# Experts: two tiles' products made in the gates' stage; mixer: convolution passes between the chunks' reads

## The chip, the cores and the metric

The kernel runs on one core of one Trainium2 chip. Its engines are TensorE (PE), VectorE (DVE), ScalarE (ACT), GpSimd (POOL) and SyncE (SP). The metric is the time of one execution on the device, in microseconds (us); less is better.

## The reference

One layer on a stream `x` of 8 x 512 x 128 float32 (4096 tokens): attention, experts, mixer, experts again. Each adds to the stream. The change touches the last three.

```
x = x + attention(layernorm(x))          # 16 heads of 64, rel. positions, top-k, 3 powers
x = x + experts(layernorm(x))            # top-1 of 8 experts, capacity tokens / 8
x = x + mixer(layernorm(x))
x = x + experts(layernorm(x))

# experts: logits = xt @ wg; mask = one_hot(argmax); drop the tokens beyond the capacity
#          gate = sum(softmax * mask); out = gate * (W[e] @ x + b[e])

# mixer:   z, xBC, dt = split(u @ W_in.T)
#          xBC = silu(causal convolution of 4 taps over time (xBC) + conv_b)
#          x, B, C = split(xBC)            # 128, 16, 16 channels; 8 heads of 16
#          y = ssd(x * dt, A * dt, B, C)   # chunks of time, decays inside, states between them
#          y = concat(y + x * Dskip, z); layernorm; out = y @ W_out.T
```

## The kernel before

Tokens lie in 32 tiles of 128. `k.X` is the stream, `k.XNT` the normed stream, transposed. Every engine runs its own program in its own order, written out by hand; semaphores join them. `bank` is PSUM: `ps[0]` to `ps[7]`, each 128 x 512. The program is a row of stages (`nc.Block`); each ends when all engines have reached its end.

**Experts** (`experts`, run twice) has two stages. In the *gates' stage* VectorE derives for all tiles the winning expert, its place in the queue and the gate (`b.gate8`). TensorE takes part once: when the mask is there (`step`) it multiplies it with `r.after` and `r.ones` into `ps[4]` and `ps[5]`, and VectorE goes on from these to the last gate (L1230 to L1238). In the *products' stage* TensorE multiplies each tile with all 8 expert matrices, as two products of 128 x 512: `q = 0` (experts 0 to 3, "near") and `q = 1` (4 to 7, "far"). Tile t uses banks 0 and 1 for even t, 2 and 3 for odd t. VectorE scales the near half with the gates (L1351), ScalarE the far half (L1314), VectorE adds them (L1343), GpSimd sums over experts and adds to the stream. Between the products TensorE transposes the gates of four tiles (`turn_gates`, L1259; ScalarE keeps them, L1302) and makes the bias product from them (L1282).

**Mixer** (`mixer`): the main stage walks over 8 batches of 512 tokens, each of 4 chunks of 128. One *step* has batch `front` enter (projections, convolution, silu), batch `cur` in its chunks, batch `back` in its norm and output, and `done` in the norm for the experts. On TensorE a chunk c has a `first_half` (the decays' differences, L1561, then the *transposes* of x and B and the product of B and C into bank `T1`, L1569 to L1571) and a `second_half` (L1580, L1584). TensorE's order in a step:

```
first_half 0, project x z bc, first_half 1, mean, second_half 0, from_start, first_half 2,
output, second_half 1, turn, first_half 3, second_half 2, square_sums, second_half 3,
logits, from_states
```

On VectorE `before(cur, c)`, the *chunk's read*, takes chunk c out of `T1` (L1843 to L1849; the last of them raises `turned_used`, on which the transposes of chunk c + 1 wait) and then multiplies the decays by the result, in two instructions L1853 (`weights`, on which `second_half` c waits). `convolution(front)` makes 4 taps for x and for B and C together, so 8 instructions (L1815 for tap 0, L1818 for taps 1 to 3). ScalarE turns the last tap's sums into tanh and half (`squash`, L1722, L1723), and VectorE makes of them silu (L1828 to L1833), on which the transposes of the next step's chunk 0 wait. GpSimd in a step: `spread` 2, the squares, `spread` 3, `spread` 0 of the next batch, `bias`, rstd, `spread` 1.

Of the kernel before, what the change touches and what calls it, by code (L numbers as in the profile page):

```python
# [16 lines left out]
P = 128  # L17
# [37 lines left out]
def bcast(ap, dims):  # L55

    return bass.AP(ap.tensor, ap.offset, [list(ap.ap[0])] + [list(d) for d in dims])
# [1026 lines left out]
CONV = 4  # L1084
# [63 lines left out]
def experts(nc, sem, sb, ps, k, r, tag, made=None, follow=None, gw=None, out=None, logits=None):  # L1148
    def S(n):
        return sem(f"{tag}_{n}")  # L1150
# [4 lines left out]
    near_made, far_made, far_scaled, near_scaled = (S(n) for n in ("near_made", "far_made", "far_scaled", "near_scaled"))  # L1155
# [27 lines left out]
    def v3(x):  # L1183
        return x[:, :].rearrange("p (t e) -> p t e", e=E)

    def over(x):

        return bcast(x[:, :], [[1, TILES], [0, E]])

    with nc.Block() as block:  # L1190
        @block.tensor
        def _(pe):
            pe.wait_ge(step, 1)
            nc.tensor.matmul(ps[4][:, 0:n8], r.after[:, :], b.mask[:, :], start=True, stop=True)
            nc.tensor.matmul(ps[5][:, 0:n8], r.ones[:, :], b.mask[:, :], start=True, stop=True).then_inc(counted, 1)

        @block.scalar
        def _(act):
            act.wait_ge(ex_done, 1)
            nc.scalar.activation(b.exp[:, :], b.diff[:, :], ACT.Exp).then_inc(ex_done, 1)  # L1200

        @block.vector
        def _(dve):
            chain = [0]

            def link(ins):

                chain[0] += 1
                ins.then_inc(gates, 1)
                dve.wait_ge(gates, chain[0])  # L1210

            link(nc.vector.memset(b.sum_b[:, :], 1.0))
            link(nc.vector.memset(b.sum_b[:, :].rearrange("p (e t) -> p e t", e=E)[:, :, 0:1], 0.0))
            if logits is None:
                dve.wait_ge(made.products, GROUPS)
                link(nc.vector.tensor_copy(b.logit[:, :], ps[3][:, 0:n8]))
            link(nc.vector.tensor_reduce(out=b.top[:, :], in_=v3(b.logit), axis=AX.X, op=ALU.max))
            nc.vector.tensor_tensor(v3(b.diff), v3(b.logit), over(b.top), ALU.subtract).then_inc(ex_done, 1)

            link(nc.vector.tensor_tensor(v3(b.same), v3(b.logit), over(b.top), ALU.is_equal))  # L1220
            link(nc.vector.tensor_tensor(v3(b.score), v3(b.same), bcast(r.rank[:, :], [[0, TILES], [1, E]]), ALU.mult))
            link(nc.vector.tensor_reduce(out=b.best[:, :], in_=v3(b.score), axis=AX.X, op=ALU.max))
            nc.vector.tensor_tensor(v3(b.mask), v3(b.score), over(b.best), ALU.is_equal).then_inc(step, 1)

            dve.wait_ge(ex_done, 2)
            link(nc.vector.tensor_reduce(out=b.total[:, :], in_=v3(b.exp), axis=AX.X, op=ALU.add))
            link(nc.vector.reciprocal(b.prob[:, :], b.total[:, :]))

            dve.wait_ge(counted, 1)
            link(nc.vector.tensor_copy(b.prev[:, :].rearrange("p (e t) -> p e t", e=E),  # L1230
                                       ps[5][:, 0:n8].rearrange("p (t e) -> p e t", e=E)))
            link(nc.vector.tensor_tensor_scan(out=b.sum_a[:, :], data0=b.sum_b[:, :], data1=b.prev[:, :],
                                              initial=0.0, op0=ALU.mult, op1=ALU.add))
            link(nc.vector.tensor_tensor(v3(b.loc), b.sum_a[:, :].rearrange("p (e t) -> p t e", e=E),
                                         ps[4][:, 0:n8].rearrange("p (t e) -> p t e", e=E), ALU.subtract))
            link(nc.vector.scalar_tensor_tensor(out=b.keep[:, :], in0=b.loc[:, :], scalar=float(CAP), in1=b.mask[:, :],
                                                op0=ALU.is_le, op1=ALU.mult))
            link(nc.vector.tensor_tensor(v3(b.gate8), v3(b.keep), over(b.prob), ALU.mult))  # L1238
# [3 lines left out]
    with nc.Block() as block:  # L1242
# [9 lines left out]
        @block.tensor  # L1252
        def _(pe):
            def turn_gates(i):
                if i:
                    pe.wait_ge(g_kept, i)
                for c in range(4):
                    at = (i * 4 + c) * E
                    last = nc.tensor.transpose(GT[0:E, c * P:(c + 1) * P], b.gate8[:, at:at + E], k.ident[:, :])  # L1259
                last.then_inc(g_turned, 1)  # L1260

            def late(i):
                group_turn(nc, pe, follow, i, gw.xn[:, i % 2, :], TURN, k.ident, 1)

            for i in range(GROUPS):
                par = i % 2
                if i == 0:
                    turn_gates(0)
                for c in range(4):
                    t = i * 4 + c  # L1270
                    for q in range(2):
                        if t >= 2:
                            pe.wait_ge((near_scaled, far_scaled)[q], t - 1)
                        nc.tensor.matmul(ps[2 * (c % 2) + q][:, :], k.XNT[:, t * P:(t + 1) * P],  # L1274
                                         r.we[:, q * 512:(q + 1) * 512], start=True, stop=True)\
                            .then_inc((near_made, far_made)[q], 1)
                    if c == 0:
                        pe.wait_ge(g_kept, i + 1)
                        if i:
                            pe.wait_ge(bias_added, i)  # L1280
                        for cc in range(4):
                            last = nc.tensor.matmul(BIAS[:, cc * P:(cc + 1) * P], gt[par][:, cc * P:(cc + 1) * P],  # L1282
                                                    r.eb[:, :], start=True, stop=True)
                        last.then_inc(bias_made, 1)
                    if c == 1 and follow and i >= 2:
                        late(i - 2)
                    if c == 2 and i + 1 < GROUPS:
                        turn_gates(i + 1)
                    if c == 3 and follow and i >= 2:
                        group_products(nc, pe, follow, i - 2, follow.W, k.XNT, EIGHT)  # L1290
            if follow:
                for i in range(GROUPS - 2, GROUPS):
                    late(i)
                    group_products(nc, pe, follow, i, follow.W, k.XNT, EIGHT)
# [97 lines left out]
def mixer(nc, sem, sb, ps, k, r, made, follow, gw):  # L1392
# [137 lines left out]
    with nc.Block() as block:  # L1530
# [264 lines left out]
        def _(dve):  # L1795
# [9 lines left out]
                ins.then_inc(m.link, 1)  # L1805
                return links[0]

            def convolution(j):

                at = {}  # L1810
                for tap in range(CONV):
                    for which, src, acc, weight in (("x", xp, cx, r.cwx), ("bc", bp, cb, r.cwb)):
                        if tap == 0:
                            dve.wait_ge(m.conv_in, j * 3 + (1 if which == "x" else 2))
                            done = nc.vector.tensor_scalar(acc[0][:, :], src[:, 0:N], weight[:, 0:1], None, ALU.mult)  # L1815
                        else:
                            dve.wait_ge(m.link, at[which])
                            done = nc.vector.scalar_tensor_tensor(  # L1818
                                out=acc[tap % 2][:, :], in0=src[:, tap:tap + N], scalar=weight[:, tap:tap + 1],
                                in1=acc[1 - tap % 2][:, :], op0=ALU.mult, op1=ALU.add)  # L1820
                        if tap < CONV - 1:
                            at[which] = link(done)
                        else:
                            done.then_inc(m.conv_out, 1)
# [82 lines left out]
            def body(front, cur, back, done):  # L1907
                if cur is not None:
                    before(cur, 0)
                    before(cur, 1)  # L1910
                if back is not None:
                    center(back)
                if front is not None:
                    convolution(front)
                if cur is not None:
                    before(cur, 2)
                    before(cur, 3)
                    states(cur)
                if back is not None:
                    variance(back)  # L1920
                if front is not None:
                    silu(front)
                if back is not None:
                    into_stream(back)
                if cur is not None:
                    add_up(cur)

            run_steps(body)


# [106 lines left out]
```

## Time and profile before

| | us |
|---|---|
| median of 3 runs (2867.4 to 2874.39) | 2870.75 |
| profiled execution | 2866.37 |
| its span | 2864.6 |
| to the first gates' stage (attention) | 2347.9 |
| the mixer's main stage | 2460.9 to 2775.3 |
| second gates' stage | 2775.3 to 2783.8 |
| second products' stage | 2783.8 to 2864.6 |

Times in the rows count from the start of the span. PE's float32 products show as two records each, so "x4" on L1274 is two products; the transposes of L1569 show as one. "PEclk" is the clock granted to TensorE as a share of 2.4 GHz: 1.00 or 0.50 (1.2 GHz).

### The profile page before, as it was taken

The page shows a single profiled execution, that of the slowest core. Times are in us where ns is not written, and L with a number is a line of the kernel's source. Part 1 is how long each engine was busy: PE and PEld are TensorE (multiplying, and loading weights), DVE is VectorE, ACT ScalarE, POOL GpSimd, SP SyncE. Part 2 cuts the span into 40 slices and gives each one's busy share as a digit, 9 for nine tenths or more (in the row PEclk, how much of TensorE's full clock was granted, in tenths as well). Part 3 has the DMA queues.
Part 4 walks back from the last instruction along what each step waited for, and adds up shares of the span by engine and source line. Part 5 has one row for each costly group of instructions (what it writes and reads, how often), then busy time and mean ns, then how long its engine had stood idle before and what let it go on. Part 6 is the DMA issues. An engine that isn't in the chain of part 4 may idle for free. (4 is left out here: it accounts for less than half of the span.)

```text
span 2864.6 us, 54829 instructions
## 1 busy us (share of the span) xinstructions
PE 2455.1 (86%) x16162; PEld 1364.4 (48%) x16162; DVE 2640.0 (92%) x6343; ACT 2072.3 (72%) x6299; POOL 2322.1 (81%) x2900
## 2 busy tenths in 40 slices
PE   5888888888888888888888888888888879588878
PEld 3444444544444444444444444444444445355544
DVE  7999999999999999999999999999999937577747
ACT  3788888888888888888888888888888736333325
POOL 5899999999999999999999999999999936344425
PEclk8899999999999999999999999999999979677769
DMA  4444444444444444444444444444444300000001
GB/s 128 118 122 118 118 119 121 124 123 118 120 124 118 123 120 118 119 125 125 119 118 122 118 123 120 123 119 124 121 125 118 100 15 1 1 1 1 1 1 30
DMA packets 367800, 279.65 MB, mean 98 GB/s; under 512 B 27590, under 2 KB 366608, under 8 KB 367504
## 3 DMA queue, kind: packets, MB, share of 16 engines
q1 hardware_dynamic: 366576, 274.06, 33.8%
q8 instruction: 131, 2.15, 0.3%
q10 hardware_dynamic: 928, 2.10, 0.3%
q14 instruction: 165, 1.35, 0.2%
HBM read 139.48 MB, written 136.58 MB: 96 GB/s over the span
## 5 line engine op out<-in xcount | busy, mean ns | idle before, releaser
L969 DVE MAX8 top<-work 128x8 f32<-128x512 f32 x1536 | 978.3, 678 | 0.0
L978 DVE MATCH_REPLACE8 work<-top,work 128x512 f32<-128x512 f32 x1024 | 684.4, 676 | 0.0
L1055 POOL TENSOR_TENSOR scores<-scores,cut 128x512 f32<-128x512 f32 x512 | 643.3, 1278 | 0.0
L588 PE MATMUL bank<-probs_t,u 128*64 128x512 f32 x2048 | 470.9, 602 | 11.5 <-ACT u L824 1.8
L1047 POOL TENSOR_SCALAR cut<-scores,minus_max_and_least 128x512 f32<-128x512 f32 x512 | 355.7, 695 | 46.9
L876 ACT ACTIVATE probs_of_tile<-scores,minus_max_and_least 128x512 f32<-128x512 f32 x512 | 376.4, 765 | 16.1 <-POOL scores L1055 16.0
L1068 POOL TENSOR_SCALAR probs_of_tile<-probs_of_tile,inverse 128x512 f32<-128x512 f32 x512 | 350.7, 696 | 26.9 <-DVE inverse L935 1.4
L978 DVE MATCH_REPLACE8 work<-top,scores 128x512 f32<-128x512 f32 x512 | 342.1, 676 | 0.0
L966 DVE MAX8 top<-scores 128x8 f32<-128x512 f32 x512 | 324.9, 676 | 1.1 <-ACT scores L817 1.0
L1051 POOL TENSOR_SCALAR cut<-cut 128x512 f32<-128x512 f32 x512 | 306.6, 615 | 21.6
L795 ACT ACTIVATE band<-band 128x129 f32<-128x129 f32 x512 | 155.1, 304 | 215.2 <-DMA band<-probs_scratch 214.9
L817 ACT ACTIVATE scores<-bank 128x512 f32<-128x512 f32 x512 | 274.0, 585 | 48.2 <-PE bank L637 48.1
L841 ACT ACTIVATE probs_t<-bank 128x512 f32<-128x512 f32 x512 | 281.3, 609 | 8.4 <-PE bank L684 7.4
L684 PE MATMUL bank<-identity,probs_of_tile 128*128 128x128 f32 x2048 | 273.7, 278 | 2.7 <-POOL probs_of_tile L1068 2.7
L672 PE MATMUL bank<-identity,band 128*128 128x128 f32 x512 | 109.2, 295 | 179.2 <-ACT band L804 178.2
L588 PEld LDWEIGHTS bank<-probs_t,u 128*64 128x64 f32 x2048 | 136.5, 137 | 263.9 <-issue 222.7
L588 PE MATMUL bank<-probs_t,v 128*64 128x384 f32 (+1 forms) x2048 | 255.3, 392 | 0.0
L684 PEld LDWEIGHTS bank<-identity,probs_of_tile 128*128 128x128 f32 x2048 | 238.6, 144 | 3.1 <-POOL probs_of_tile L1068 3.1
L588 PEld LDWEIGHTS bank<-probs_t,v 128*64 128x64 f32 x2048 | 124.3, 139 | 172.6 <-ACT probs_t L841 98.7
L609 PE MATMUL bank<-keys_left,qt 64*128 64x64 f32 (+3 forms) x1024 | 186.0, 440 | 1.5 <-ACT scores L817 1.4
L854 ACT ACTIVATE rel<-bank 128x254 f32<-128x254 f32 x512 | 174.4, 413 | 1.9 <-PE bank L625 1.9
L1021 POOL TENSOR_TENSOR res<-res,tmp 128x512 f32<-128x512 f32 x128 | 163.5, 1278 | 10.7
(281 smaller groups left out, 4753.4 us busy)
## 6 DMA issues: line engine op xcount, KB each, us to landing
probs_scratch<-probs_of_tile SPq DMA_DIRECT2D x256, 256.0 KB, 2.5
band<-probs_scratch SPq DMA_DIRECT2D x256, 256.0 KB, 3.1
rel_scratch<-rel SPq DMA_DIRECT2D x256, 254.0 KB, 3.0
relj<-rel_scratch SPq DMA_DIRECT2D x256, 128.0 KB, 2.3
relj<-rel_scratch SPq DMA_DIRECT2D x512, 64.0 KB, 2.4
stream<-in_L_attn_a_x SPq DMA_DIRECT2D x4, 512.0 KB, 8.8
out_stream<-stream SPq DMA_DIRECT2D x8, 256.0 KB, 2.3
wout_rows<-in_L_attn_a_Wout ACTq DMA_DIRECT2D x1, 512.0 KB, 11.8
```

Of the source, the lines that this page charges most:

```text
L588: last = nc.tensor.matmul(U[HEADS[h], lo:hi], lhs, pt[mpar][:, h, jt, lo:hi], start=(jt == 0 and lo == 0), stop=(jt == NT - 1 and step > 0))
L684: last = nc.tensor.transpose(PT[h][:, jt * P:(jt + 1) * P], t.prob[Td][:, h, HALF + jt * P:HALF + (jt + 1) * P], k.ident[:, :])
L817: nc.scalar.activation(sc[Tb][:, h, :], SC[h][:, :], ACT.Copy).then_inc(s.scores_kept, 1)
L841: nc.scalar.activation(pt[dpar][:, h, :, Td * P:(Td + 1) * P], PT[h][:, :].rearrange("p (j i) -> p j i", j=NT), ACT.Copy).then_inc(s.probs ...
L876: nc.scalar.activation(t.prob[Tx][:, h, HALF:HALF + N], sc[Tx][:, h, :], ACT.Exp, bias=neg[q][:, h, 0:1], accum_out=rs[Tx][:, h:h + 1]).th ...
L966: nc.vector.max(top[q][:, h, 0:8], sc[Tc][:, h, :]).then_inc(s.tops, 1)
L969: nc.vector.max(top[q][:, h, 8 * rnd:8 * rnd + 8], work[:, h, :]).then_inc(s.next_tops, 1)
L978: nc.vector.match_replace(out=work[:, h, :], in_to_replace=top[q][:, h, 8 * rnd:8 * rnd + 8], in_values=sc[Tc][:, h, :] if rnd == 0 else w ...
L1047: nc.gpsimd.tensor_scalar(cut[:, h, :], sc[Tc][:, h, :], neg[q][:, h, 1:2], STEEP, ALU.add, ALU.mult).then_inc(s.compared, 1)
L1051: nc.gpsimd.tensor_scalar(cut[:, h, :], cut[:, h, :], 0.0, NEG, ALU.min, ALU.max).then_inc(s.cut, 1)
L1055: nc.gpsimd.tensor_tensor(sc[Tc][:, h, :], sc[Tc][:, h, :], cut[:, h, :], ALU.add).then_inc(s.masked, 1)
L1068: nc.gpsimd.tensor_scalar(row, row, inv[Ty][:, h:h + 1], 1.0, ALU.mult, ALU.mult).then_inc(s.probs, 1)
```

## The change

In the gates' stage TensorE makes the four products of tiles 0 and 1 behind its two products of the mask, and the products' stage begins with tile 2's. In the mixer VectorE makes taps 0 and 1 where it made all four; tap 2 follows the read of chunk 2 and tap 3 the read of chunk 3.

```diff
@@ experts, gates' stage, TensorE
             nc.tensor.matmul(ps[5][:, 0:n8], r.ones[:, :], b.mask[:, :], start=True, stop=True).then_inc(counted, 1)
+            for t in range(2):
+                for q in range(2):
+                    nc.tensor.matmul(ps[2 * t + q][:, :], k.XNT[:, t * P:(t + 1) * P], r.we[:, q * 512:(q + 1) * 512],
+                                     start=True, stop=True).then_inc((near_made, far_made)[q], 1)
@@ experts, products' stage, TensorE
-                    for q in range(2):
-                        if t >= 2:
-                            pe.wait_ge((near_scaled, far_scaled)[q], t - 1)
+                    for q in range(2 if t >= 2 else 0):
+                        pe.wait_ge((near_scaled, far_scaled)[q], t - 1)
@@ mixer, VectorE
-            def convolution(j):
-
-                at = {}
-                for tap in range(CONV):
+            at = {}
+
+            def convolution(j, taps):
+
+                for tap in taps:
@@ mixer, VectorE's step
                 if front is not None:
-                    convolution(front)
+                    convolution(front, (0, 1))
                 if cur is not None:
                     before(cur, 2)
+                if front is not None:
+                    convolution(front, (2,))
+                if cur is not None:
                     before(cur, 3)
+                if front is not None:
+                    convolution(front, (3,))
+                if cur is not None:
                     states(cur)
```

TensorE at the seam of the two expert stages, before (L1194 and L1195 are the mask's products, the branches are the stages' seam, L1259 the gates' transposes, L1274 the tiles' products, L1282 the bias):

```order
L1194 MATMUL bank<-experts_mask,rest_after 128x256
L1195 MATMUL bank<-experts_mask,rest_ones 128x256
L1190 UNCONDITIONAL_BRANCH
L1252 UNCONDITIONAL_BRANCH
L1259 MATMUL bank<-identity,experts_gate 8x128 x4
L1274 MATMUL bank<-rest_we,stream_normed_t 128x512 x2
L1282 MATMUL bank<-rest_eb,experts_gt 128x128 x4
L1274 MATMUL bank<-rest_we,stream_normed_t 128x512 x4
```

The same place of the changed kernel, where L1198 is the new line, L1263 the gates' transposes, L1285 the bias and L1277 the tiles' products:

```order
L1194 MATMUL bank<-experts_mask,rest_after 128x256
L1195 MATMUL bank<-experts_mask,rest_ones 128x256
L1198 MATMUL bank<-rest_we,stream_normed_t 128x512 x4
L1190 UNCONDITIONAL_BRANCH
L1256 UNCONDITIONAL_BRANCH
L1263 MATMUL bank<-identity,experts_gate 8x128 x4
L1285 MATMUL bank<-rest_eb,experts_gt 128x128 x4
L1277 MATMUL bank<-rest_we,stream_normed_t 128x512 x2
```

Four products have moved from behind the seam to ahead of it; the bias product, which waits for ScalarE, now stands directly behind the gates' transposes.

VectorE in the middle of a mixer step, before, from the last of the centering to the read of chunk 3:

```order
L1887 TENSOR_TENSOR mixer_z<-mixer_z,bank 128x512
L1815 TENSOR_SCALAR mixer_sum_x<-mixer_conv_x,rest_cwx 128x512
L1815 TENSOR_SCALAR mixer_sum_bc<-mixer_conv_bc,rest_cwb 64x512
L1818 SCALAR_TENSOR_TENSOR mixer_sum_x<-mixer_conv_x,rest_cwx,mixer_sum_x 128x512
L1818 SCALAR_TENSOR_TENSOR mixer_sum_bc<-mixer_conv_bc,rest_cwb,mixer_sum_bc 64x512
L1818 SCALAR_TENSOR_TENSOR mixer_sum_x<-mixer_conv_x,rest_cwx,mixer_sum_x 128x512
L1818 SCALAR_TENSOR_TENSOR mixer_sum_bc<-mixer_conv_bc,rest_cwb,mixer_sum_bc 64x512
L1818 SCALAR_TENSOR_TENSOR mixer_sum_x<-mixer_conv_x,rest_cwx,mixer_sum_x 128x512
L1818 SCALAR_TENSOR_TENSOR mixer_sum_bc<-mixer_conv_bc,rest_cwb,mixer_sum_bc 64x512
L1843 COPY mixer_b_rows<-bank 128x16
L1844 TENSOR_TENSOR mixer_cb<-bank,rest_upto 128x128
```

The changed kernel from the second instruction of tap 1 to tap 3 (L1822 is a tap, L1847 to L1857 a chunk's read):

```order
L1822 SCALAR_TENSOR_TENSOR mixer_sum_bc<-mixer_conv_bc,rest_cwb,mixer_sum_bc 64x512
L1847 COPY mixer_b_rows<-bank 128x16
L1848 TENSOR_TENSOR mixer_cb<-bank,rest_upto 128x128
L1851 TENSOR_TENSOR mixer_dtx<-bank,mixer_dt 128x4x2x16
L1853 TENSOR_TENSOR mixer_dtx_end<-bank,mixer_dt_to_end 128x128
L1857 TENSOR_TENSOR mixer_weights<-mixer_decay,mixer_cb 128x512 x2
L1822 SCALAR_TENSOR_TENSOR mixer_sum_x<-mixer_conv_x,rest_cwx,mixer_sum_x 128x512
L1822 SCALAR_TENSOR_TENSOR mixer_sum_bc<-mixer_conv_bc,rest_cwb,mixer_sum_bc 64x512
L1847 COPY mixer_b_rows<-bank 128x16
L1848 TENSOR_TENSOR mixer_cb<-bank,rest_upto 128x128
L1851 TENSOR_TENSOR mixer_dtx<-bank,mixer_dt 128x4x2x16
L1853 TENSOR_TENSOR mixer_dtx_end<-bank,mixer_dt_to_end 128x128
```

The read of chunk 2 has passed ahead of four convolution instructions, the read of chunk 3 ahead of two, and the states behind it come two instructions later. No instruction is added or dropped on VectorE, ScalarE or GpSimd.

## Rows read from the trace of the kernel before

**Rows 1.** Windows by stage: us from the start, length, busy us of each engine, PEclk

```profile
2460.90:2775.30 314.40, 264.05 (x1344) 155.76 (x1344) 217.40 (x467) 94.67 (x184) 128.51 (x96) 0.74 0.00 1
2783.80:2864.60 80.80, 71.03 (x224) 34.14 (x224) 53.91 (x72) 40.28 (x136) 42.55 (x24) 0.94 0.09 27
```

**Rows 2.** Timeline, the second seam of the expert stages: start us, us, engine, line

```profile
2779.43 1.06 PE L1195 MATMUL bank<-experts_mask,rest_ones 128*128 128x256 f32 x2
...
2782.86 0.43 DVE L1238 TENSOR_TENSOR experts_gate<-experts_keep,experts_prob 128x256 f32<-128x256 f32 x1
...
2783.83 1.01 PE L1259 MATMUL bank<-identity,experts_gate 128*8 128x128 f32 x4 [3.34 <-PEq L1190]
...
2784.63 3.62 PE L1274 MATMUL bank<-rest_we,stream_normed_t 128*128 128x512 f32 x4
2784.87 0.59 ACT L1302 ACTIVATE experts_gt<-bank 8x512 f32<-8x512 f32 x1 [7.78 <-PE bank L1259]
...
2788.18 1.22 PE L1282 MATMUL bank<-rest_eb,experts_gt 8*128 8x128 f32 x8
...
2789.33 3.70 PE L1274 MATMUL bank<-rest_we,stream_normed_t 128*128 128x512 f32 x8
```

**Rows 3.** Windows in the products' stages (two answers: second stage, first stage)

```profile
2783.80:2788.30 4.50, 4.47 (x9) 1.70 (x9) 0.69 (x1) 0.60 (x2) 0.00 (x0) 0.50 0.00 0
2788.30:2854.80 66.50, 66.50 (x216) 32.44 (x216) 52.01 (x70) 38.53 (x131) 37.69 (x21) 1.00 0.08 25
...
2361.70:2436.00 74.30, 74.30 (x288) 40.00 (x287) 57.87 (x126) 50.67 (x164) 49.27 (x48) 1.00 0.00 1
```

**Rows 4.** Waits in the mixer (total us, times, longest), and the window of one step

```profile
PE bank L1569 <- DVE mixer_dtx_end L1849: 27.9, 7, 5.6
...
2575.00:2613.00 38.00, 34.30 (x170) 20.34 (x169) 27.47 (x59) 11.79 (x23) 16.65 (x13) 0.72 0.00 1
```

**Rows 5.** Timeline of PE in the step of 2575 to 2613

```profile
2595.70 1.88 PE L1561 MATMUL bank<-mixer_a_spread,rest_after 128*128 128x512 f32 x4
2601.27 0.48 PE L1569 MATMUL bank<-identity,mixer_x 128*128 128x128 f32 x1 [3.68 <-DVE mixer_dtx_end L1849]
...
2615.51 0.42 PE L1569 MATMUL bank<-identity,mixer_x 128*128 128x128 f32 x1
```

**Rows 6.** Timeline of DVE in the same step

```profile
2589.83 0.48 DVE L1815 TENSOR_SCALAR mixer_sum_x<-mixer_conv_x,rest_cwx 128x512 f32<-128x512 f32 x1
...
2593.52 2.38 DVE L1818 SCALAR_TENSOR_TENSOR mixer_sum_x<-mixer_conv_x,rest_cwx,mixer_sum_x 128x512 f32<-128x512 f32 x1
...
2599.80 0.73 DVE L1818 SCALAR_TENSOR_TENSOR mixer_sum_bc<-mixer_conv_bc,rest_cwb,mixer_sum_bc 64x512 f32<-64x512 f32 x1
...
2600.94 0.27 DVE L1849 TENSOR_TENSOR mixer_dtx_end<-bank,mixer_dt_to_end 128x128 f32<-128x128 f32 x1
...
2602.61 0.17 DVE L1843 COPY mixer_b_rows<-bank 128x16 f32<-128x16 f32 x1
...
2603.41 1.29 DVE L1853 TENSOR_TENSOR mixer_weights<-mixer_decay,mixer_cb 128x512 f32<-128x512 f32 x2
...
2609.12 0.69 DVE L1833 SCALAR_TENSOR_TENSOR mixer_x<-mixer_tanh_x,mixer_half_x 128x512 f32<-128x512 f32 x1
```

**Rows 7.** Timeline of POOL in the same step

```profile
2593.01 4.64 POOL L1759 TENSOR_TENSOR mixer_a_spread<-rest_upto,mixer_a 128x1024 f32<-128x1024 f32 x2
2597.61 1.71 POOL L1771 TENSOR_TENSOR stream<-stream,mixer_out_bias 128x512 f32<-128x512 f32 x1
```

**Rows 8.** Groups of instructions in the mixer: count, busy us, mean ns

```profile
L1853 DVE TENSOR_TENSOR mixer_weights<-mixer_decay,mixer_cb 128x512 f32<-128x512 f32 x64 | 44.4, 736 | 1.1
```

**Rows 9.** Windows: PE's small products in the same step, and in the last full step

```profile
2601.30:2616.70 15.40, 15.38 (x77) 10.98 (x77) 10.67 (x32) 2.31 (x5) 6.20 (x7) 0.50 0.00 0
2743.90:2750.40 6.50, 6.50 (x70) 5.07 (x68) 3.70 (x13) 1.28 (x3) 1.02 (x1) 1.00 0.01 3
```

**Rows 10.** Timeline of ACT in the same step, the last of the squash

```profile
2601.76 0.71 ACT L1723 ACTIVATE mixer_half_bc<-mixer_sum_bc,rest_cbb 64x512 f32<-64x512 f32 x1
```

## Prediction

> **What bounds the kernel now.** I read the windows by stage first. The change touches only what lies behind the attention: two expert runs and the mixer, whose main stage is 314 us long [rows 1]. In the products' stage of the second experts the windows show TensorE busy 66.50 of 66.50 us, and 74.30 of 74.30 in the first [rows 3]: TensorE sets the pace from the first tile to the last, and the chain that ended last runs through its L1274 too. What is taken from TensorE ahead of that stretch should come off the end, us for us.
>
> In the mixer no engine is full: in the step of 2575 to 2613 TensorE works 34.30 of 38.00 us, VectorE 27.47, GpSimd 16.65 [rows 4]. So I read the waits and followed one step. TensorE ends the decays' differences of chunk 3 at 2597.6 and stands 3.68 us, until 2601.27, for VectorE's L1849, the read of chunk 2 [rows 5]. VectorE had been in the convolution from 2589.83 to 2600.53, 10.7 us, and read chunk 2 only then [rows 6]. From 2601.27 TensorE works without a stop into the next step, where VectorE waits for it. So a step is a ring: TensorE from chunk 3's transposes to chunk 1's, VectorE from chunk 1's read through the convolution to chunk 2's. The wait occurs 7 times, once in each step that has both a batch in its chunks and one entering, and sums to 27.9 us [rows 4].
>
> **The seams of the experts.** Gone from the products' stage: two products at the half clock, 3.62 us, and two at the full one, half of 3.70. Tile 2's first product starts now at 2789.33 + 1.73 = 2791.06 [rows 2].
>
> The four moved products can start where the mask's end, 2779.43 + 1.06 = 2780.49. VectorE needs its own time to 2783.29 for the gates, and the next stage begins 0.54 later [rows 2]. So 2.8 us of the four lie under VectorE's chain; the rest holds up the seam, since a stage ends when all its engines have. Bounds: all at the full clock 4 x 0.86 = 3.4 us, end 2783.9; all at the half clock 4 x 1.71 = 6.9 us, end 2787.4. Between: before, the granted clock was 0.50 for the first 4.50 us in which TensorE ran without a stop [rows 3]. Its run now begins with the mask's first product, near 2778.4. If the clock rises 4.5 us on again, at 2782.9, 2.4 us of the products pass at the half clock (1.4 products) and 2.6 products at the full one in 2.2 us: end 2785.1, stage 2785.65. Behind it come the gates' transposes at the full clock (0.5), ScalarE's copy (0.59, with its waits 0.65) and the bias (1.1): tile 2's first product at about 2787.9. The far half of tile 0 is scaled by then, since ScalarE needs 1.2 us behind its copy. Gain 3.2 us; with the bounds for the end 4.4 and 0.9. Twice: **6.4 us**, between 1.8 and 8.8. No DMA is issued or moved in these stages. The banks 2 and 3 are free, the logits in bank 3 having been copied before the mask is made.
>
> **The mixer.** No instruction is added. Taps 2 and 3 are what stood from 2593.52 to 2600.53, 7.0 us [rows 6]. With them behind it, the read of chunk 2 starts at 2593.6, and L1849 is done near 2594.5 in place of 2601.2. TensorE itself comes to the transposes at 2597.6 [rows 5]. So of 7.0 us the ring can use 3.68, and over 7 waits 27.9 [rows 4]; then TensorE is the bound.
>
> What is late next: the read's two L1853 now fall among GpSimd's spreads (2593.01 to 2597.65) and `bias` [rows 7]. The L1818 of 2593.52 took 2.38 us beside a spread and the one of 2599.80 took 0.73 alone [rows 6], so a wait of 1.65. Does L1853 wait like this? Its 64 have a mean of 736 ns [rows 8]: by that alone they don't, but few of them stood beside a spread. The Trainium skill, "SBUF — State Buffer", section "SBUF: two separate sides", says that a VectorE instruction with two SBUF inputs and a GpSimd instruction exclude each other for their whole length, whoever starts first. By that both L1853 wait and the mixer's gain is the smaller of the two sums below; without it, the larger. I go by the L1818, which reads two tiles of SBUF as L1853 does: the first L1853 done at 2596.0, the second near 2598.4, tap 2 with the rest of `bias` at 2600.9, and chunk 3's read (2602.61 to 2604.70, so 2.1 us [rows 6]) ends at 2603.0. Chunk 2's second half, wanted at 2598.3, does not wait. Chunk 3's second half, behind the square sums, is wanted at 2602.7 if these run at the half clock (3.5 us) and at 2601.0 at the full one, so it waits 0.3 to 2.0 us. Now these products all ran at the half clock, behind TensorE's standing; in the last full step, in which TensorE had not stood, they ran at the full one [rows 9]. So I lean to the upper end: 1.5 us. Sum: 27.9 - 7 x 1.5 = **17.4 us**; without L1853's waits 27.9, with 2.0 each 13.9.
>
> Hidden: tap 3 is now the last thing before the states. Now silu ends at 2609.81 and the next transposes of chunk 0, which wait for it, start at 2615.51 [rows 5, 6], so 5.7 us lie free. Tap 3 will end at 2603.0 + 1.4 = 2604.4, 3.9 us later than 2600.53: covered by 1.8 us. Behind tap 3 on ScalarE stand only the logits' copy and the next decays, whose differences come later. GpSimd's order is the same.
>
> **The sum.** 6.4 + 17.4 = 23.8 us off 2866.37, the profiled execution, makes 2842.6. That execution was 4.4 below the median of the runs, 2870.75, so I forecast 2870.75 - 23.8 = 2847.0.
>
> **The rivals.**
> - *The clock stays up in the mixer* (0.13). In 15.4 us of small products from 2601.3 on the clock was 0.50 although TensorE was busy 15.38 of them; in the last step 6.50 us of the like ran at 1.00 [rows 9]. If ending the standing keeps the clock up through all of it, half of the 15.4 goes too. Then VectorE and ScalarE bound the step: tap 3's end for x at 2603.7, the squash, which now ends at 2602.47 [rows 10], 2.6 us behind the last x pass, silu 2.1, so the next chunk 0 at 2608.5 in place of 2615.5: 7.0 us a step, 49 in all, and 2870.75 - 6.4 - 49 = 2815. Against: the small products hold the clock down as long as they last, whatever came before.
> - *GpSimd gives the wait back* (0.17). VectorE's reads queue behind spreads, squares and bias, the second halves wait 3 us or more, and the mixer gains 0 to 6. With 1.8 to 6.4 from the experts: 2859 to 2869. For it: 2.38 against 0.73 us.
> - *Slower* (0.06): tap 3, queued behind chunk 3's read, makes silu late, in the next step's chunk 0. It decides from where tap 3 ends later than 2604.4 + 1.8 = 2606.2, so from two more blocked instructions (3.3 us) on. With the experts' gain the time is above 2876 once each of the 7 steps loses 1.7 us beyond that, or four blocked instructions; five (8.3 us, 6.5 beyond, 45 in all) would make 2910.
> - *The moved products hold up the seam fully* (inside the forecast): the end at 2787.4 gives 1.8 instead of 6.4 us, 2851.6.
> - *My sum* (0.64): 2836 to 2858.
>
> **How the numbers follow.** The measurement tells about 0.2%, 5.7 us, from no change. Faster by more is below 2865.0: the sum, the first rival and most of the second, 0.64 + 0.13 + 0.10 = 0.87. Same: 0.08. Slower: 0.05. The range takes in all of the sum's bounds (27.9 + 8.8 gives 2834; 0 + 8.8 gives 2862), part of the first rival's way down, and leaves out its end and the slower side: 2831 to 2861.
>
> **What would show it.** Right: the wait of L1569 for L1849 gone or below 1 us; the interleaved L1853 at 1.3 to 2.4 us; L1818 of tap 2 and 3 nearer 0.73; a short wait of L1584 or L1580 for L1853; steps of 34 to 35 us for 37.7; in the experts the stage's end 1 to 3 us behind L1238, and no product of tile 0 behind the seam. Wrong: steps that stay at 37 us with the wait at L1584, or a wait of L1569 for silu.

## The result, and the profile after

The changed kernel takes 2826.63 us (median of 4 runs, 2821.12 to 2835.61), the kernel before 2872.57 us on the same chip: a ratio of 0.9844, 95% interval 0.9808 to 0.9879, so 45 us less (35 to 55). I had forecast 24 less, and a time between 2831 and 2861. The profiled execution took 2821.94, its span is 2820.2: 44.4 us below that of before.

The windows of the changed kernel by stage (columns as in [rows 1]), the mixer's main stage, the second gates' stage and the second products' stage:

```profile
2457.50:2734.60 277.10, 237.03 (x1344) 139.30 (x1344) 228.68 (x467) 94.07 (x184) 123.81 (x96) 0.80 0.00 1
2744.20:2820.20 76.00, 65.49 (x216) 32.02 (x216) 49.63 (x72) 40.00 (x136) 44.33 (x24) 0.95 0.10 28
2734.60:2744.20 9.60, 5.98 (x12) 3.07 (x12) 6.03 (x15) 0.42 (x1) 0.00 (x0) 0.67 0.00 0
```

The mixer's stage went from 314.4 to 277.1 us [rows 1] and its granted clock from 0.74 to 0.80. The first number behind the length is TensorE's busy time, for 1344 records both times: 264.05 us before, 237.03 now. So of the 37.3 us, 27.0 are the same instructions done in less time, and 10.3 (50.35 to 40.07) are idle time gone. The gates' stage grew by about 1 us, the products' stage lost 4.8.

Inside the mixer I time the steps by VectorE's last addition of a batch, which comes once a step; its first and last start stand in a row. Before and after:

```profile
L1880 DVE TENSOR_TENSOR mixer_y<-mixer_y,mixer_y_from_states x8: 557/559/560, 2504.9 to 2753.7; 128x384 f32<-128x384 f32 x8
```
```profile
L1884 DVE TENSOR_TENSOR mixer_y<-mixer_y,mixer_y_from_states x8: 557/558/559, 2501.5 to 2713.5; 128x384 f32<-128x384 f32 x8
```

The seven intervals between these eight took 248.8 us and take 212.0, 36.8 less, where I had 17.4. In them TensorE's busy time fell by 27.1 us (222.74 to 195.60) and its idle time by 9.7. A full step went from 37.6 to 30.6 us. The seam of the second experts on TensorE, first the start of before, then the changed kernel:

```profile
2778.41 1.22 PE L1194 MATMUL bank<-experts_mask,rest_after 128*128 128x256 f32 x2 [3.71 <-DVE experts_mask L1223]
```
```profile
2737.97 1.22 PE L1194 MATMUL bank<-experts_mask,rest_after 128*128 128x256 f32 x2 [3.71 <-DVE experts_mask L1227]
...
2739.84 4.12 PE L1198 MATMUL bank<-rest_we,stream_normed_t 128*128 128x512 f32 x8
2744.28 0.60 PE L1263 MATMUL bank<-identity,experts_gate 128*8 128x128 f32 x4 [0.32 <-PEq L1190]
2745.55 1.15 PE L1285 MATMUL bank<-rest_eb,experts_gt 8*128 8x128 f32 x8 [0.68 <-ACT experts_gt L1305]
2746.63 1.98 PE L1277 MATMUL bank<-rest_we,stream_normed_t 128*128 128x512 f32 x4
```

From the mask's first product to tile 2's first product it is 8.66 us. Before it was 12.65: from 2778.41 to 2791.06, which is 2789.33 and the 1.73 us of tile 1's two products [rows 2]. That is 4.0 us here, and another 4.0 at the first seam. 36.8 + 8.0 is 44.8, close to the 44.4 us between the spans.

The waits in the mixer:

```profile
DVE mixer_b_rows L1847 <- PE bank L1574: 18.4, 10, 5.6
PE bank L1587 <- DVE mixer_weights L1857: 11.1, 7, 1.9
```

The wait of the transposes for the read of chunk 2 (27.9 us, 7 times [rows 4]) is nearly gone (0.31 us once, 0.37 once), and the second half of chunk 3 waits instead: 11.1 us, 7 times, where I had 7 x 1.5 = 10.5. VectorE's own waits for TensorE's transposes, the other half of the ring, fell from 60.5 to 18.4 us. So the waits that I had looked at came out as forecast. TensorE's idle time fell by less than their 16.8 us, 10.3 in the stage, since other waits came, the longest in the first two steps (2.50 us for chunk 2's `weights`, twice 1.66 for the states). What the forecast lacks is in the busy time, and the clock shows where. Here is one step of before, cut at the changes of the clock, and one of after:

```profile
2583.60:2600.50 16.90, 13.99 (x88) 7.83 (x86) 13.84 (x17) 7.54 (x15) 9.33 (x5) 1.00 0.00 1
2600.70:2621.00 20.30, 19.71 (x81) 12.46 (x82) 13.30 (x41) 4.05 (x8) 7.19 (x7) 0.50 0.00 0
```
```profile
2597.60:2617.90 20.30, 19.89 (x131) 11.67 (x130) 19.80 (x38) 8.24 (x17) 12.78 (x10) 1.00 0.01 2
2618.10:2628.10 10.00, 8.95 (x38) 5.79 (x38) 9.31 (x21) 3.35 (x7) 2.89 (x2) 0.50 0.00 0
```

Before, TensorE ran at the half clock for 20 us of each full step, from inside its standing on; now for 10 us. The arithmetic of a full step: the standing 3.68 -> 1.58 saves 2.1 us. TensorE's busy time is 13.99 + 19.71 = 33.70 us before and 19.89 + 8.95 = 28.84 after, 4.9 less; half of the 10.3 us less at the half clock is 5.1. Together 7.0 to 7.2, and 7.0 are measured. The experiments ask whether the standing is indeed the cause of the lower clock, and what bounds the step now.

### The profile page after: what moved, and what is told of

Read it like the earlier page. It is cut to its first block and busy times, and to the rows that moved or that the text cites. A ratio compares the mean times of both kernels' runs of the same rounds, so it can differ in the third digit from the quotient of the medians.

```text
span 2820.2 us, 54829 instructions
## 1 busy us (share of the span) xinstructions
PE 2429.9 (86%) x16162; PEld 1351.5 (48%) x16162; DVE 2646.9 (94%) x6343; ACT 2069.9 (73%) x6299; POOL 2313.1 (82%) x2900
## 5 line engine op out<-in xcount | busy, mean ns | idle before, releaser
L969 DVE MAX8 top<-work 128x8 f32<-128x512 f32 x1536 | 993.4, 698 | 0.0
L978 DVE MATCH_REPLACE8 work<-top,work 128x512 f32<-128x512 f32 x1024 | 694.4, 696 | 0.0
L1021 POOL TENSOR_TENSOR res<-res,tmp 128x512 f32<-128x512 f32 x128 | 163.3, 1276 | 10.7
```

The source lines that it names most:

```text
L969: nc.vector.max(top[q][:, h, 8 * rnd:8 * rnd + 8], work[:, h, :]).then_inc(s.next_tops, 1)
L978: nc.vector.match_replace(out=work[:, h, :], in_to_replace=top[q][:, h, 8 * rnd:8 * rnd + 8], in_values=sc[Tc][:, h, :] if rnd == 0 else w ...
```

## The experiments

The kernels ran in four groups, the last three each on a chip of its own, each group with the kernel before beside them, so medians of different groups can't be compared. The gains are worked out from each ratio and the median of the kernel before in that group (2865 to 2873 us). They are known to about 4 us, that of the changed kernel to 10, so a difference of a few microseconds between two gains is noise. "Steps" are the seven intervals of the rows above in the one profiled execution. They repeat well where the mixer is the same (248.8, 249.2 and 249.2; 212.0 and 212.0), so small differences are read from them. The profiled execution of the kernel with 198.5 was its slowest, 2814.27 us.

| kernel | median us | ratio (95%) | gain us | steps us |
|---|---|---|---|---|
| changed kernel | 2826.63 | 0.9844 (0.9808 to 0.9879) | 45 | 212.0 |
| mixer alone | 2826.65 | 0.9864 (0.9851 to 0.9878) | 39.0 | 212.0 |
| experts alone | 2857.69 | 0.9971 (0.9959 to 0.9983) | 8.3 | 249.2 |
| before, standing filled | 2846.42 | 0.9930 (0.9918 to 0.9943) | 20.1 | 232.6 |
| same, two more | 2843.71 | 0.9927 (0.9915 to 0.9940) | 20.9 | 226.0 |
| changed, standing added | 2837.33 | 0.9902 (0.9889 to 0.9916) | 28.1 | 227.3 |
| before, seam filled | 2862.50 | 0.9988 (0.9979 to 0.9997) | 3.4 | 249.2 |
| changed, filled | 2821.58 | 0.9842 (0.9828 to 0.9855) | 45.3 | 209.5 |
| changed, filled twice | 2817.12 | 0.9827 (0.9814 to 0.9840) | 49.6 | 206.8 |
| changed, squares on ScalarE | 2816.40 | 0.9831 (0.9818 to 0.9844) | 48.4 | 206.2 |
| same, and one spread | 2811.17 | 0.9809 (0.9795 to 0.9822) | 54.7 | 201.3 |
| same, filled | 2806.59 | 0.9793 (0.9779 to 0.9808) | 59.3 | 198.5 |
| same, filled twice | 2802.48 | 0.9781 (0.9767 to 0.9794) | 62.7 | 191.4 |

**The two parts alone.** The mixer's hunks of the diff alone, and the experts' hunks alone.

> The mixer's part of the change alone; the experts' seams are as before. In the two traces the steps of the mixer account for 36.6 us (37.2, 33.3, 37.9, 37.7, 37.6, 37.6 and 27.5 us before, 36.9, 30.3, 30.5, 30.6, 30.7, 30.7 and 22.5 after) and the two seams for 8.0. Theory of the clock (shorter standing, and because of it less time at the half clock): the two parts are separate, so 36 to 37 us off the kernel before, and the step's window at half clock is 10 us as in the changed kernel. Rival, that the parts help each other (the experts' earlier rise of the clock, or the attention's end, plays into the mixer): clearly less than 36, and a half-clock stretch nearer the 20.5 us of before.

> The experts' part alone, the mixer as before. Read from the two traces: from the mask's first product to tile 2's first product 12.8 and 12.65 us before, 8.75 and 8.66 after, so 8.0 us off in all, where I had forecast 6.4. If the seams gain by themselves: 7.5 to 8.5 us off the kernel before. If the forecast's 6.4 was right and the rest came from the mixer: 6 to 7 us.

39.0 and 8.3 us, the steps 212.0 as in the changed kernel: the parts are separate and add up, within the error. In the trace of the experts alone the second seam gained 3.9 us and the first 3.1: there the four products took 5.15 us in place of 4.21, and the granted clock rose near 2353.9, 3.1 us into them (1.2 us into them in the changed kernel). So a seam is worth 3.1 to 4.0, and 7 to 8 in all.

**The standing of before filled.** The order of VectorE and all waits stay; TensorE works on nothing instead of standing.

```diff
@@ first_half, ahead of the wait for turned_used
+                if c == 3 and j < B - 1:
+                    pe.wait_ge(m.conv_in, (j + 1) * 3 + 3)
+                    for _ in range(4):
+                        nc.tensor.matmul(PZ[:, :], r.ones[:, :], r.we[:, 0:512], start=True, stop=True)
```

> The kernel before with one addition: where TensorE stands for VectorE's read of chunk 2, it makes four more products of 128x512 into the free bank of z, whose result nobody reads. The order of VectorE and the wait of the transposes are those of the kernel before. Theory of the clock: the standing of 3.7 us is what drops TensorE to half clock for 20.5 us of each step; with the standing filled, the clock stays up, the small products behind the read run at the full clock, and a step gets shorter by 4 to 7 us, 28 to 49 in all, although not one instruction of VectorE has moved. Rival, that VectorE's order alone brought the gain (the read comes earlier, the clock is a by-product or is held down by the small products): no gain, 0 to 5 us slower for the added products.

20.1 us (16.2 in the steps), without moving an instruction of VectorE and with empty work added. The rival is out; my 28 to 49 us were too high. The windows of one step, of the small products behind the read, and of what follows:

```profile
2567.20:2601.20 34.00, 33.23 (x178) 18.40 (x178) 27.24 (x59) 11.79 (x24) 16.48 (x13) 0.85 0.00 1
...
2595.30:2601.20 5.90, 5.37 (x64) 4.61 (x65) 5.70 (x16) 1.39 (x3) 1.02 (x1) 1.00 0.01 3
2601.20:2611.40 10.20, 10.20 (x19) 4.32 (x19) 7.09 (x23) 2.11 (x5) 6.12 (x7) 0.50 0.00 0
```

The small products just behind the read, which ran at the half clock in [rows 9], run at the full one. But the clock falls all the same, 5.9 us into them, and TensorE paused there only briefly, as the waits of the mixer's stage show:

```profile
PE bank L1573 <- DVE mixer_dtx_end L1853: 3.9, 7, 2.2
PE bank L1584 <- DVE mixer_weights L1857: 3.6, 7, 0.5
```

In this step the two pauses were 0.25 and 0.52 us. So the standing started the half clock early, and small products can bring it without one. Half of the 10.1 us less at the half clock is 5.1, a step lost 3.6 (37.6 to 34.0): TensorE, added products and all, is busy 33.23 of 34.00 us and is what bounds it.

**A standing put into the changed kernel.** Chunk 3's transposes also wait for tap 2.

```diff
@@ first_half, ahead of the wait for turned_used
+                if c == 3 and j < B - 1:
+                    pe.wait_ge(m.link, 7 * (j + 1) + 6)
```

> The changed kernel with one wait more: the transposes of chunk 3 also wait for the end of tap 2, so TensorE stands there some 3 us. VectorE's order is that of the changed kernel, and its read of chunk 3, which begins behind tap 2 in any case, comes about 1.0 us later (the length of the transposes and the product behind them). Rival, the order alone: 1 to 2 us a step, 7 to 14 in all. Theory of the clock: the standing brings the half clock back for 20 us of the step in place of 10, which costs 5 us more: 5 to 7 us a step, 35 to 50 us in all, so about the time of the kernel before.

```profile
2588.20:2622.30 34.10, 31.10 (x169) 19.45 (x169) 29.20 (x58) 11.79 (x23) 16.13 (x12) 0.80 0.00 1
2588.20:2601.80 13.60, 13.60 (x72) 10.34 (x73) 11.64 (x31) 2.75 (x5) 3.98 (x5) 0.50 0.00 0
2602.00:2622.30 20.30, 17.30 (x98) 9.11 (x96) 17.35 (x28) 9.03 (x18) 11.95 (x8) 1.00 0.01 1
```

17 us slower than the changed kernel (28.1 for 45 of gain), 15.3 in the steps: between the two forecasts. In a full step (3.5 us longer) the half clock lasts 13.6 us, not the 20 I expected and not the 10 of the changed kernel. TensorE's busy time in the step went from 28.9 to 31.10 us, so 2.2 us are the clock's, and its idle time from 1.7 to 3.00, so 1.3 are the wait's. Half of the added half-clock time would be 1.7 only: the changed kernel's stretch held 1.05 us of idle time, this one none, and only busy time is made longer. With a standing of 3.0 us in place of 3.68 the half clock is not back at 20 us: its length doesn't follow from the standing's alone.

**Fillers in the changed kernel.** First the pair ahead of the square sums, then also the one ahead of the logits.

```diff
@@ TensorE's step
+                if front is not None and cur is not None:
+                    for _ in range(2):
+                        nc.tensor.matmul(PZ[:, :], r.ones[:, :], r.we[:, 0:512], start=True, stop=True)
                 if back is not None:
                     square_sums(back)
                 if cur is not None:
                     second_half(cur, 3)
+                if front is not None and cur is not None:
+                    for _ in range(2):
+                        nc.tensor.matmul(DF[0][:, :], r.ones[:, :], r.we[:, 0:512], start=True, stop=True)
                 if done is not None:
                     logits(done)
```

> The changed kernel with two more products of 128x512, read by nobody, ahead of the square sums, so that TensorE has no standing left ahead of chunk 3's second half (1.58 us in the step of 2599 to 2630). Theory A, that a standing is what drops the clock: no half-clock stretch is left in the full steps (10.2 us now), TensorE gets 5 us of slack, and VectorE, which idles 0.8 of 30.6 us, is the bound: 0 to 5 us faster in all, no more. Theory B, that the small products (square sums, second halves, logits, 128x128 and narrower) drop it also without a standing, as the filled kernel before hints (its clock fell at 2601.2 behind 6 us of small products with pauses of 0.25 and 0.52 only): a half-clock stretch of 10 us stays in each step, and the time is that of the changed kernel within 2 us.

> As the last, and two more such products ahead of the logits, so that wide products stand among the small ones. Under theory B this, unlike the last, takes the half-clock stretch away in full steps; under theory A it adds nothing to it. In time both say little (VectorE is the bound): within 5 us of the changed kernel, and if the added 1.7 us a step lie on the path, up to 12 slower. The clock of the step's windows tells.

The first leaves half-clock stretches of 3.4 to 10.1 us and takes 2.5 us off the steps. But it does not leave TensorE without a standing, as I had expected: with the wait ahead of chunk 3's second half filled, TensorE stands behind the logits, for the states, and in this step the clock fell at 2586.7, inside that standing:

```profile
2587.18 1.65 PE L1594 MATMUL bank<-mixer_c,mixer_states 16*128 16x128 f32 x6 [1.05 <-DVE mixer_states L1878]
```

The second, whose window over more than five steps this is, has no half clock left:

```profile
2534.00:2700.00 166.00, 156.42 (x992) 91.41 (x990) 157.94 (x314) 63.08 (x124) 84.45 (x65) 1.00 0.00 1
```

Four wide products a step keep the clock up. Which theory that supports stays open: the second pair stands among the small products, as B asks, but it also fills the standing for the states, and TensorE stands 0.85 us later in the step instead, ahead of chunk 0's transposes, without a fall of the clock. For B speaks the filled kernel before, whose clock fell behind pauses of 0.25 and 0.52 us only. In time the second pair is worth 2.7 us in the steps (4.3 by the gains), since VectorE is busy 157.94 of the 166 us. In the changed kernel the rest of the half clock is nearly free.

Two more products in the filled kernel before, likewise ahead of the logits:

> The kernel before with the four added products of the earlier run where TensorE stands, and two more ahead of the logits, among the small products. With the first four alone the clock still fell for 10.2 us in each step, behind the small products, and the step went from 37.7 to about 34.1 us. If the small products hold the clock down and wide ones among them prevent it, as in the filled changed kernel (167 us at full clock without a break), the half-clock stretch goes here too and its 10.2 us become 5.1, less the 1.7 us of the two added products: 0 to 3.4 us a step, 0 to 24 us off the earlier run. If nothing is left to win because the ring of reads and transposes is the bound: within 3 us of the earlier run.

The half-clock stretch went from 10.2 to 6.7 us (0.50 from 2594.20 to 2600.90). It begins in the square sums, ahead of the added pair, which itself ran at the half clock: a wide pair behind the fall shortens the stretch and does not prevent it. The full step stayed at 34.1 us with TensorE busy 33.33 of it: what the clock gave, the added work took. The gains differ by 0.8 us, within the error. The steps are 6.6 us shorter in the trace, nearly all of it in the first (31.6 for 36.6 us) and the last (24.0 for 25.7), for which I have no explanation.

**VectorE's waits for GpSimd.** In the changed kernel's step VectorE and GpSimd read:

```profile
2607.97 0.73 DVE L1822 SCALAR_TENSOR_TENSOR mixer_sum_x<-mixer_conv_x,rest_cwx,mixer_sum_x 128x512 f32<-128x512 f32 x1
2608.63 1.52 DVE L1822 SCALAR_TENSOR_TENSOR mixer_sum_bc<-mixer_conv_bc,rest_cwb,mixer_sum_bc 64x512 f32<-64x512 f32 x1
...
2610.86 3.90 DVE L1857 TENSOR_TENSOR mixer_weights<-mixer_decay,mixer_cb 128x512 f32<-128x512 f32 x2
...
2617.81 1.29 DVE L1857 TENSOR_TENSOR mixer_weights<-mixer_decay,mixer_cb 128x512 f32<-128x512 f32 x2
```
```profile
2607.73 1.88 POOL L1769 TENSOR_TENSOR mixer_square_z<-mixer_z 128x512 f32<-128x512 f32 x1
2609.57 4.64 POOL L1762 TENSOR_TENSOR mixer_a_spread<-rest_upto,mixer_a 128x1024 f32<-128x1024 f32 x2
```

The read of chunk 2 has come in beside the two spreads and takes 3.90 us for 1.29. Two experiments take work off GpSimd: the squares alone, then also the spread of chunk 3.

```diff
@@ ScalarE, behind decays(cur, 2); the same lines leave GpSimd's step
+            def spread3(j):
+                t = j * NT + 3
+                act.wait_ge(m.diffs, t - 1)
+                for h in range(MH):
+                    last = nc.scalar.activation(al[1][:, h, :], r.upto[:, :], ACT.Copy,
+                                                scale=b.a[:, t * MH + h:t * MH + h + 1])
+                last.then_inc(m.spread3, 1)
+            def squares(j):
+                act.wait_ge(m.centered, j + 1)
+                for e, of in enumerate((yt[j % 2], zt[j % 3])):
+                    last = nc.scalar.activation(sq[e][:, :], of[:, :], ACT.Square)
```

> The changed kernel with GpSimd's squares and its spread of chunk 3 made on ScalarE (two squares, and eight instructions of 128x128 for the spread), so that less of GpSimd stands beside VectorE's instructions with two SBUF inputs. In the changed kernel's step VectorE's instructions are longer beside GpSimd's than alone by about 8 us: 2.51 and 3.90 against 1.29 for L1857, 1.26 against 0.48 for tap 0, 1.52 and 1.75 against 0.73 for taps 1 and 2, 2.34 against 0.68 for silu; 4 to 5 of them are beside the squares and the two spreads. Theory that VectorE bounds the step through these waits: L1857 of chunk 2 near 1.3 to 2.5, and the steps shorter by 1.7 (TensorE's own 28.9 us are then the bound) to 4 us, so 12 to 28 us in all. Rival, that TensorE at half clock is the bound already: under 1 us a step, within 6 us of the changed kernel.

> The changed kernel with the two squares alone moved from GpSimd to ScalarE; all four spreads of a step stay on GpSimd. With both moved the mixer's seven steps gained 10.7 us on the changed kernel. Beside the squares the bc pass of tap 0 took 1.26 in place of 0.48 us and that of tap 1 1.52 in place of 0.73: if only overlap counts, 1.5 us a step, 10 us in all, and the spread had no part. If what counts is what stands beside the read of chunk 2 (3.90 us for its L1857), the spreads, free earlier, move but stay beside VectorE's work and the gain is 0 to 5 us.

Together 9.9 us off the changed kernel (54.7 of gain for 44.8; 10.7 in the steps), under the 12 of my lower end; the squares alone 3.6 (5.8 in the steps), near the 0 to 5 of the second forecast. In gains alone neither is clear of the changed kernel's error of 10 us; the steps are. With both moved VectorE's busy time in the steps fell from 193.5 to 171.8 us and TensorE's from 195.6 to 193.9: TensorE, busy 193.9 of 201.3 us, is the bound now, so not all of VectorE's 21.7 us count. So these waits cost time, and about half of what the steps gained (4.9 of 10.7 us) came with the spread. The groups of L1857 in the changed kernel and, as L1868, with both moved:

```profile
L1857 DVE TENSOR_TENSOR mixer_weights<-mixer_decay,mixer_cb 128x512 f32<-128x512 f32 x64 | 69.2, 1121 | 1.1
```
```profile
L1868 DVE TENSOR_TENSOR mixer_weights<-mixer_decay,mixer_cb 128x512 f32<-128x512 f32 x64 | 60.7, 988 | 1.1
```

**Both bounds at once.** ScalarE's share with one pair of fillers, and with both.

> The same with the two added products. If the standing ahead of chunk 3's second half is what keeps a half-clock stretch in the step, both bounds are moved at once: 3 to 5 us a step, 20 to 35 us off the changed kernel. If the fill does nothing to the clock: the time of the last kernel, within 3 us.

> The kernel with squares and one spread on ScalarE, and both pairs of added products (ahead of the square sums and ahead of the logits). It takes VectorE's waits for GpSimd and TensorE's half clock away together. If each bounds a part of the step: 3 to 8 us faster than with one pair (2806.6), so near 2800. If the added products now lie on the path: within 3 us of it or slower.

The first falls short of its 20 us (14.5 against the changed kernel); the second, 2802.48 us, is the fastest kernel of the study, 2.2% below before and 17.9 us of gain beyond the changed kernel's. In the steps it is 20.6 us off the changed kernel, more than the 10.7 of ScalarE's share and the 5.2 of the two pairs add up to: each alone had run into the other's bound. (The gains say 17.9 against 9.9 and 4.8, a difference within their error.) Against one pair the second is worth 3.4 us by the gains, as forecast. Its window:

```profile
2560.00:2620.00 60.00, 60.00 (x365) 34.46 (x364) 55.46 (x124) 33.08 (x73) 20.49 (x19) 1.00 0.00 1
```

Now TensorE is the bound, at the full clock, and some of what it does is the filler.

**The seam filled.** Four empty products behind the mask's, those of tiles 0 and 1 left where they were.

```diff
@@ gates' stage, TensorE, behind the mask's products
+            for q in range(4):
+                nc.tensor.matmul(ps[q][:, :], r.ones[:, :], r.we[:, 0:512], start=True, stop=True)
```

> The kernel before with four added products of 128x512 behind the mask's, read by nobody, in both gates' stages; the products of tiles 0 and 1 stay behind the seam. It splits the seams' gain of 4.0 us each into the clock's part and the moved work's. In the changed kernel the stage behind the seam began 0.9 us later than before. Behind it the full clock turns the transposes' 1.01 us into 0.60, the first tile's two products' 3.62 into 1.85 and takes 0.1 off the bias: 2.3 us back. Clock's part alone: 2.3 - 0.9 = 1.4 us a seam, 2.8 us in all. Rival, that the clock plays no part in the seams: 0.9 us slower each, 1.8 in all.

```profile
2781.93 4.22 PE L1197 MATMUL bank<-rest_we,rest_ones 128*128 128x512 f32 x8
2786.45 0.60 PE L1261 MATMUL bank<-identity,experts_gate 128*8 128x128 f32 x4 [0.30 <-PEq L1190]
2786.88 1.88 PE L1276 MATMUL bank<-rest_we,stream_normed_t 128*128 128x512 f32 x4
```

3.4 us (0.9 to 6.0), 2.8 expected: transposes 0.60 for 1.01, two products 1.88 for 3.62 [rows 2]. The traces, from the mask's first product to tile 1's first, give 1.1 and 1.2 us a seam. So about 1.2 of a seam's 4.0 us are the clock's; the rest is work that lies under VectorE's chain.

## Why the prediction was wrong

- **The mixer's sum had no term for the clock.** The step that failed is "TensorE is the bound" with "27.9 - 7 x 1.5 = 17.4 us": it took only the standing off and left TensorE's busy time as it was. That busy time fell by 27.0 us for the same 1344 records, 27.1 of the 36.8 us of the seven intervals: it is what the shorter half clock gave back. Filling the standing of before and moving nothing won 20.1 us, 16.2 in the steps. The windows that I showed held it: 0.50 right behind the standing [rows 9]. I used that row to size the new wait and then priced the clock at "nothing or all".
- **The wait's own term was right in its parts and too high in sum.** The wait that went (27.9) and the one that came (11.1 for 10.5) make 16.8 us, but TensorE's idle time fell by 10.3 only. In the first step its 5.61 us of standing turned into other waits (0.31, 2.50, 1.86 and 1.66 us, for 0.67 and 0.33 before), so TensorE's idle time there hardly changed.
- **The argument against the first rival was wrong**: "the small products hold the clock down as long as they last, whatever came before". With the standing filled they ran at the full clock for 5.9 us, in the changed kernel the square sums and chunk 2's second half did. Half of it was right: they can bring the half clock on without a longer standing. The rival, at 0.13, said 7.0 us a step with VectorE and ScalarE as the next bound; a full step gained 7.0, with VectorE busy 29.4 of 30.6 us. That the number fits is in part luck: the rival had the clock up through all the small products and VectorE free of GpSimd's waits, while 10 us of half clock stayed and those waits grew. The time came out at 2827, not 2815, because the first two intervals and the last gained less (0.3, 3.1 and 5.0 us).
- **L1857 waits behind the spreads: right.** I had the pair of chunk 2 take 4.8 us (2593.6 to 2598.4); it took 3.90, chunk 3's 1.29. The Trainium skill, "SBUF — State Buffer", section "SBUF: two separate sides", calls the ports that the two engines share an exclusive lock. The trace agrees: tap 1's bc pass took 1.52 us beside a square, tap 2's 0.73 alone. What I had as hidden became the bound: L1857's total grew by 24.8 us (44.4 [rows 8] to 69.2) while that of taps 1 to 3 fell by 22.2 (71.7 to 49.5): the waits for GpSimd moved along with the order, and with VectorE busy 29.4 of 30.6 us they now count.
- **Tap 3's slack: right.** Silu ends at 2626.17, the transposes of chunk 0 start at 2627.14, behind TensorE's own differences.
- **The price of the half clock.** The Trainium skill, "TensorE: Matmul & The Clock Gate", section "HAM oscillation — how this bites in real kernels", charges half of the throttled time. The changed kernel agrees: 10.3 us less at the half clock, TensorE's busy time 4.9 us less. Where TensorE is not the bound the step doesn't get that back: taking away what half clock the changed kernel with one pair still had won 2.7 us over seven steps (4.3 by the gains), under 1 us a step.
- **The seams: right mechanism, 8.0 us for 6.4.** The clock rose earlier than I had put it: the four products took 4.1 to 4.2 us, not 4.6, the seam was delayed by 0.9 us, not 1.85, and the stage began 0.3 us behind them, not 0.54.
- **The other rivals.** GpSimd did not give the wait back; the second halves wait 1.6, not 3 us. Silu was not late: no wait of the transposes for it came beyond the one of 6.99 us in the first step, which both kernels have. In the rival "slower" a sum was wrong: 1.7 us beyond the slack of 1.8 takes three blocked instructions (3 x 1.65 = 4.95 us), not four. And the range was said to hold all of the sum's bounds, but its end of 2861 leaves out the 2862. Neither decided anything.

What stays open: what exactly brings the half clock behind the small products. It came behind pauses of 0.25 and 0.52 us, and four wide products a step prevented it in the changed kernel; whether by their width or by the standing of 1.05 us that they filled is not shown.

## What to carry to other kernels

When a stall of TensorE is removed, read the granted clock behind it: the sum has two terms, the stall and half of TensorE's busy time at the half clock that it started, up to the next engine's bound. The cheapest test is to fill the stall with empty products and change nothing else; it shows in one run that part of the stall's cost is the clock (here 16 to 20 us, of the 27 that the change itself got back). Behind any change, compare TensorE's busy time for the same instructions: the clock's part stands there by itself. And before VectorE's work is moved, look at what GpSimd does at its new place, since the wait between them moves along.

## What the runs showed of the hardware that I had not expected

- Empty work made a kernel faster: four products of 128x512 a step, 20.1 us (16.3 to 23.5) off 2866.
- TensorE, with pauses of 0.25 and 0.52 us, still fell to the half clock behind 5.9 us of small products; with two pairs of wide products added to each step the changed kernel held the full clock for 166 us.
- A low tile does not spare VectorE the wait for GpSimd. L1834 reads and writes 16 partitions; it took 0.68 us in all eight batches of the kernel before and 2.34 in most of the changed kernel's. That is as long as tap 2's x pass of 128 partitions took beside a spread, 2.38 [rows 6]:

```profile
L1834 DVE SCALAR_TENSOR_TENSOR mixer_c<-mixer_tanh_bc,mixer_half_bc x8: 678/2341/2347, 2471.0 to 2684.4; 16x512 f32<-16x512 f32 x8
```
